# Two attention layers in a loop over the batch: where the loop's semaphores are cleared

## What is computed

```python
# layer 0 (h = context and latents, one after the other)
attn = softmax(where(full_mask, einsum('bkhd,bnhd->bhkn', q, kmat) / DH, -inf))
attn_out = einsum('bhkn,bnhd->bkhd', attn, v).reshape(b, k_len, H) @ out_w + out_b + residual
out = rmsnorm(attn_out, postnorm_w)
x = gelu(out @ mlp_w1 + mlp_b1) @ mlp_w2 + mlp_b2 + residual
# layer 1
scores = einsum('bkgld,bksd->bkgls', q, k) * scale + encoder_attention_mask
out = einsum('bkgls,bksd->bkgld', softmax(scores), v) @ Wo + bo
x = out + hidden_state
return (x - mu) * rsqrt(var + EPS) * gamma + beta
```

## Time and profile before

| | us |
|---|---|
| median of 3 runs | 4206.88 (4205.88 to 4209.81) |
| the profiled execution, its time | 4201.49 |
| the profiled execution, its span | 4199.8 |
| TensorE busy | 3795.2 (90% of the span), mean granted clock 0.956 |
| VectorE, ScalarE, GpSimd busy | 2531.5, 2255.2, 2061.6 |

### The profile page before, as it was taken

The page is one execution under the profiler, slowest core; times in us unless marked ns, Lnnn a source line. Parts: engine busy times, 40 slices in busy tenths (PEclk is TensorE's granted clock), DMA queues, the critical chain, the costliest instruction groups (busy, mean ns, idle before and its releaser), DMA issues. The chain is left out here.

```text
span 4199.8 us, 56149 instructions
## 1 busy us (share of the span) xinstructions
PE 3795.2 (90%) x18688; PEld 1900.2 (45%) x18688; DVE 2531.5 (60%) x6933; ACT 2255.2 (54%) x2656; POOL 2061.6 (49%) x996
## 2 busy tenths in 40 slices
PE   8999969997899996999789999699978999969997
PEld 4444644442444464444244447444424444644442
DVE  3565547884356554788435655478843565547884
ACT  0556218885055611888505552288850555118885
POOL 0667017664066701767406670176640667017674
PEclk9999979999999997999999999799999999979999
DMA  4222421110422132111042223211104122321110
GB/s 118 42 52 48 143 64 21 21 21 11 118 42 52 48 139 68 21 21 21 11 118 42 52 49 143 64 21 21 21 11 118 42 52 50 138 67 21 21 21 11
DMA packets 104003, 226.74 MB, mean 54 GB/s; under 512 B 23429, under 2 KB 44677, under 8 KB 94985
## 3 DMA queue, kind: packets, MB, share of 16 engines
q1 hardware_dynamic: 99272, 217.61, 21.5%
q10 hardware_dynamic: 4416, 5.30, 0.5%
HBM read 117.13 MB, written 4.19 MB: 29 GB/s over the span
## 5 line engine op out<-in xcount | busy, mean ns | idle before, releaser
L1085 POOL TENSOR_TENSOR l_pt<-l_pt,l_maskT 128x1024 f32<-128x1024 f32 x448 | 1068.9, 2393 | 479.2 <-ACT l_pt L1107 479.2
L1148 DVE CUSTOM_DVE_ANT_0 tile_b<-l_psR,hT 128x400 f32<-128x400 f32 (+1 forms) x2048 | 1065.3, 571 | 390.2 <-PE l_psR L1223 388.8
L498 DVE TENSOR_REDUCE l_acc<-l_psR 128x1 f32<-128x424 f32 (+1 forms) x1280 | 704.0, 590 | 386.6 <-PE l_psR L578 378.6
L470 ACT ACTIVATE l_pt<-l_psB 128x1024 f32<-128x1024 f32 (+1 forms) x576 | 554.1, 976 | 249.9 <-PE l_psB L600 192.3
L1223 PE MATMUL l_psR<-split_w,qst 64*128 64x400 f32 (+1 forms) x2048 | 553.2, 452 | 137.3 <-PEq L1336 118.3
L1121 ACT ACTIVATE l_pt<-l_pt 128x1024 f32<-128x1024 f32 (+1 forms) x512 | 532.9, 1055 | 25.8 <-POOL l_pt L1085 22.0
L1223 PEld LDWEIGHTS l_psR<-split_w,qst 64*128 64x128 f32 x2048 | 257.0, 192 | 614.1 <-DVE l_acc L1148 375.5
L578 PE MATMUL l_psR<-l_kst,l_qst 128*128 128x424 f32 (+1 forms) x1280 | 469.6, 411 | 12.9 <-DVE l_acc L498 8.5
L1107 ACT ACTIVATE l_pt<-l_psB 128x1024 f32<-128x1024 f32 x448 | 457.7, 1023 | 39.6 <-PE l_psB L1249 22.7
L1266 PE MATMUL l_psO<-l_pt,V 128*32 128x512 f32 (+1 forms) x3328 | 469.1, 605 | 8.0 <-ACT l_pt L1121 8.0
L1249 PE MATMUL l_psB<-qst,split_w 64*128 64x512 f32 (+1 forms) x1664 | 416.8, 424 | 5.5 <-ACT l_pt L1107 3.5
(11 more groups left out here) (145 smaller groups left out, 4570.6 us busy)
## 6 DMA issues: line engine op xcount, KB each, us to landing
l_kst<-l_khl SPq DMA_DIRECT2D x192, 264.1 KB, 3.9
mid_w<-in_w SPq DMA_DIRECT2D x128, 256.0 KB, 3.3
split_w<-k SPq DMA_DIRECT2D x192, 100.1 KB, 3.9
hT<-in_maskN SPq DMA_DIRECT2D x16, 800.5 KB, 10.6
l_qst<-l_qhl SPq DMA_DIRECT2D x192, 64.0 KB, 2.0
qst<-q SPq DMA_DIRECT2D x384, 32.0 KB
hT<-in_ctxT SPq DMA_DIRECT2D x12, 800.0 KB, 11.4
tile_c<-in_wo SPq DMA_DIRECT2D x8, 1024.0 KB, 6.3
```

The source lines that it names most:

```text
L470: act.activation(pt[0:r, n % NPT0, 0:w], psB[0:r, 2 * (n % 2):2 * (n % 2) + 2, :].rearrange("p a n -> p (a n)")[:, 0:w], ACT.Exp).then_inc ...
L498: dve.tensor_reduce(acc[:, h % 2, qt, c:c + 1], psR[:, ring[item] % NR, 0:w], AX.X, ALU.max).then_inc(s_red, 1)
L1085: pool.tensor_tensor(probabilities(n, r), probabilities(n, r), mask_of(t, r), ALU.add).then_inc(s_padd, 1)
L1148: dve.tensor_tensor_reduce(junk[:, n % 2, 0:hi - lo], bank(at)[:, 0:hi - lo], maskN[:, qt, lo:hi], 1.0, -3e38, ALU.add, ALU.max, acc[:, p ...
```

## The change

The list of 121 clears at the end of the loop body and the barrier behind it are taken out. Instead, SyncE clears in the block of layer 0 the 52 semaphores whose names begin with `l1_`, between its loads and the copies of the heads, and in the block of layer 1 the 69 semaphores that begin with `l0_` or `mid_`, between the loads of the mask tiles and the copies for later pairs. So the clears of a layer's semaphores run in a block that does not use them, and the barrier at that block's end comes before their next use. To have all `l1_` names known when the block of layer 0 is built, they are listed and allocated ahead of the loop. Behind the loop, once, the `l1_` semaphores are cleared again, since the last layer 1 has no layer 0 after it.

```diff
+L1_SEMAPHORES = ["wo_in", "maskN_in", "bc_in", "last_rows", "m_full", "a_full", "a_reduced", "nmax", "max_hi",
...
+L1_SEMAPHORES += [f"maskT_in{i}" for i in range(T1)]
...
-def layer0_attention(nc, ctx, ios, b, keep, sem):
+def layer0_attention(nc, ctx, ios, b, keep, sem, finished):
...
         sp.dma_start(wk[:, :, P:D], ios["wk0"][:, :, P:D]).then_inc(s_w, 16)
+        for s in finished:
+            sp.sem_clear(s)
         for h in range(H0):
...
-def layer1_attention(nc, ctx, ios, b, keep, sem):
+def layer1_attention(nc, ctx, ios, b, keep, sem, finished):
...
             sp.dma_start(maskT[0:r, i, :], ios["maskT"][b, t * P:t * P + r, :]).then_inc(s_mt[t], 16)
+        for s in finished:
+            sp.sem_clear(s)
         for p in range(PAIRS_OF_HEADS - 2):
...
+    def used_by(*layers):
+
+        return [s for name, s in sems.items() if name.startswith(layers)]
+
+    for name in L1_SEMAPHORES:
+        sem("l1_" + name)
...
-                layer0_attention(nc, ctx, ios, b, keep, sem)
+                layer0_attention(nc, ctx, ios, b, keep, sem, used_by("l1_"))
...
-                    layer1_attention(nc, ctx, ios, b, keep, sem)
-
-            for s in sems.values():
-                nc.sync.sem_clear(s)
-            nc.all_engine_barrier()
+                    layer1_attention(nc, ctx, ios, b, keep, sem, used_by("l0_", "mid_"))
+
+        for s in used_by("l1_"):
+            nc.sync.sem_clear(s)
```

More of the change, by code:

```diff
@@ L62 @@
 LOWEST = -3e38
+L1_SEMAPHORES = ["wo_in", "maskN_in", "bc_in", "last_rows", "m_full", "a_full", "a_reduced", "nmax", "max_hi",
+                 "max_hilo", "b_full", "masked", "exp", "pv", "maskP_bounded", "maskP_hi", "maskP_lo",
+                 "copied", "masked_by_pool", "zeros", "sums", "max_plus_hi", "osb", "rsum", "att", "max_rows",
+                 "var", "rstd", "minus_half", "o_full", "y", "norm", "out"]
+L1_SEMAPHORES += [f"k_in{i}" for i in range(2)]
+L1_SEMAPHORES += [f"q_in{i}" for i in range(SLOTS)]
+L1_SEMAPHORES += [f"maskT_in{i}" for i in range(T1)]
 RANK = {"PE": "MYXaBWAO", "DVE": "NZDTR", "ACT": "JESCP", "POOL": "G"}
```

## The result

The change makes the kernel faster: 4184.19 us (4177.69 to 4186.97, 4 runs) against 4208.35 us (4205.88 to 4211.37, 4 runs), 24.2 us less. The ratio is 0.9940 with a 95% interval from 0.9923 to 0.9957, which is 18 to 32 us. The profiled execution has a time of 4186.97 us, the longest of its four, and a span of 4185.6 us; that of before, 4201.49 us, was shorter than all four executions behind the median of before. So the two spans differ by only 14.2 us, and this difference has to be taken apart first.

A forecast was written before the change was run, and what follows sets the result against it. TensorE is busy 3795.2 of 4199.8 us, but in the seam between elements nothing else has work left, so shortening it moves everything behind. 21.75 + 4.25 = 26.0 us off 4206.9 gives 4180.9 us, range 4174.5 to 4187.5.

The forecast's parts named there:

- The seam, 3 x 7.25 = 21.75 us: Between batch elements: the clears and second barrier go, saving 7.25 us at each of three jumps back, 21.75 us.
- the jump: SyncE's branch back to its next element's first instruction, between batch elements: stays at 3.8 us.
- The end, 4.25 us: Behind the last block's barrier: 7.6 us becomes 3.2 to 3.5 us with 52 clears, saving taken as 4.25.
- The clears in the blocks, 0: 52 clears in layer 0 (2.9 us) and 69 in layer 1 (3.8 us) lie in SyncE's waits: cost 0.
- the cover: Layer 0: SyncE's 16.3 us of waits plus TensorE's 8.6 us of lead, 24.9 us before head 0 is late.
- The clock, 0 +- 1.5 us a seam: TensorE's clock still falls in the shorter seam; its return may shift each of three seams by 0 +- 1.5 us.
- the sum: Whole kernel: 21.75 + 4.25 = 26.0 us saved, against the median 4180.9 us, 0.62% less.
- the last rival: Clock's return, first load's landing or gaps inside elements shift: gain below 19.5 or above 32.5 us, 4% either side.
- The sign that did not hold: Blocks of layer 0, middle and layer 1 last as long as before within 2 us; lengthened blocks would show the forecast wrong.
- the two theories: Clears cost 55 to 60 ns only where others wait for SyncE, against clears inside blocks holding up other engines.
- That clears hold up other engines' semaphores: Rival, inside the blocks: each clear delays TensorE's chain 25 ns, 12 us in four elements; gain 14, time 4193; chance 4%.
- That clears are slow beside DMAs: Rival, layer 0: clears slow under dense DMA traffic; measurably slower from 0.65 us a clear, giving 4216; chance 2%.

The follow-up runs named there:

- The repeated profile: The changed kernel run once more, unaltered, in a second set with more rounds: 28.6 us less than before, ratio 0.9932 (0.9919 to 0.9945).
- the list of 624: The changed kernel with the clears in the block of layer 0 made twelve times: 4246.37 us, ratio to before 1.0080.
- the doubled list: The kernel before, with its list of 121 clears at the end of the loop body made twice: 4239.03 us, ratio 1.0072.

## Why the prediction was right

*The seam, 3 x 7.25 = 21.75 us.* Measured in the profile: 7.0, 7.4 and 6.8, 21.2 in sum, as the table shows. The missing 0.5 us is the jump. I had it unchanged at 3.8 us; the three jumps were 3.8, 4.0 and 3.7 us before and are 4.1, 3.8 and 4.1 after. That is the size of its scatter, or a cost of 0.2 us; the two cannot be told apart. The repeated profile has seams of the same length (4.1 to 4.4 us).

*The end, 4.25 us.* Measured 3.9. The 52 clears behind the loop take 3.4 us (4182.2 to 4185.6) and not 2.9, because they are spaced 58 ns in the median and not 55, and one pause of 0.40 us lies among them.

*The clears in the blocks, 0.* Right for both, and now shown: with four times as many the elements are as long as with one, and with twelve times as many they are late by what exceeds the cover. Only their size was off, 3.5 and 3.9 us for 52 and 69 instead of 2.9 and 3.8, and that made no difference, as they were covered. In layer 0 the margin to the first wait was 0.3 us where I expected 0.5, and to the first copy 1.6 us where I expected 3.2.

*The clock, 0 +- 1.5 us a seam.* It does still fall in the shorter seam: of the first eight matmuls behind the three seams 4 to 7 start some 0.85 us apart instead of 0.43, and 3 to 7 before. The mechanism was right, but the sum looked for the scatter in the seams alone, and only the last rival named the rest of the element. It sits in the middles as well, in steps of 1.5 us each, and in when the latents land, so that one execution's blocks can be 11 us longer than another's, and two profiles alone would have said 14 us of gain for a change worth 25.

*The sign that did not hold.* Blocks of layer 0, middle and layer 1 were to last as long as before within 2 us, and longer blocks were to speak against the forecast. In the first profile the first layer 0 is 2.6 us and the first middle 2.9 us longer than before. That margin was too narrow for what one program does by itself: the first middle alone was 184.6 us in the first profile of the changed kernel and 181.6 in the second. So the sign could not tell the two theories apart, and the kernel with four times the clears had to.

*The sum.* 26.0 us forecast, 25.1 in the seams and at the end, 24.2 and 28.6 by the medians of two sets. The forecast of 4180.9 us lies 3.3 us below the one median and 0.9 above the other. So good a hit is partly luck, since medians of the same kernel differ by 4 us. What was forecast from the parts and measured in the parts is the 25.1.

*The rivals.* That clears hold up other engines' semaphores is refuted by the kernel with four times the clears. That clears are slow beside DMAs is refuted by their spacing in layer 0, where the rival needed 650 ns: 68 ns on average in the second layer 0 of after, at a DMA share of 1.06 (1067 to 1071 us), and 61 in the list of 624. By the Trainium skill (Runtime: NRT & Kernel Launch, Instruction fetch mechanics) a taken branch to a target outside the instructions held costs a fetch; the trace agrees: five instruction packets lie in the jump, and with the loop written out they and 4.2 us a seam are gone.

## What to carry to other kernels

Time in which no engine is busy does not show on a page of busy times. Look in the timeline for the largest idle that ends in "issue", list the instructions by line in that stretch, and price the housekeeping there (a clear, a barrier, a jump, a wait for a write) by its spacing rather than by its duration. Such housekeeping costs nothing once it stands in a wait that its engine has anyway, and how much fits there is the sum of that engine's waits plus the lead of what it feeds, which can be read from the trace to within a microsecond. Compare the parts and not the spans of two profiles: here the seams repeat to 0.3 us, while the sum of the blocks differs by 7 us between two executions of one program.

## What the runs showed of the hardware

A clear lasts 25 to 30 ns and is spaced 55 ns in the list of 121 and 58 ns in the median in the changed kernel, with 25 ns and 30 ns in the median for one by itself; why the two differ was not tried. Longer lists have pauses. In the kernel with 624 clears in a row, those between two pauses are (count, durations, first and last start):

```profile
L372 SPq EVENT_SEMAPHORE_RANGE_CLEAR  x128: 25/30/37, 31.6 to 38.9; - x128
L372 SPq EVENT_SEMAPHORE_RANGE_CLEAR  x128: 25/30/37, 39.3 to 46.6; - x128
```

That list has five pauses: one of 0.49 us behind the 43rd clear, and one of 0.37 to 0.38 us after every 128 clears from there. The 52 clears of layer 0 in the changed kernel have theirs behind the 43rd too, of 0.44 to 0.48 us, and the 52 behind the loop have one of 0.40. With four times the clears the list of layer 1 pauses behind its 68th and its 196th. So the pauses come at every 128th instruction of SyncE and not at fixed times. Each is followed by a packet of instructions. From 31.2 to 58.6 us, with four pauses, there are these:

```profile
q14 instruction: 4, 0.03, 0.4%
```

They start 1.0 us behind the start of the pause, and one packet of this queue is 8 KB (161 of them are 1.32 MB in the whole trace of after), which for 128 instructions is 64 bytes each. So the pause marks the step from one block of 128 instructions to the next, and a packet with further instructions follows it. SyncE does not wait for that packet, which starts when the clears have gone on for 0.6 us. What takes the 0.4 us within the step no run shows.

The list of 121 in the kernel before has no pause, and by the doubled list one can see why: there the pause comes after exactly 128 clears, so the step lies just ahead of the first clear. The 0.4 us between the barrier and the first clear in the earlier trace rows may be this pause; a packet of instructions follows there too.

The jump back of the loop lasts 3.5 to 4.4 us on SyncE over all kernels with a loop, and GpSimd's and ScalarE's next instruction comes 3.0 to 4.4 us behind their branches, though they had waited at a barrier for 7 us before it in the kernel before. TensorE's branch instruction itself lasts 3.3 to 3.8 us where it jumps and 0.08 us at the end, where it does not. The step from one block to the next costs 0.08 us.
